# Adjacency attention in seven-product units: where the shared product stands, and in which order the tiles of a pass come

## Reference

```python
h = jnp.maximum(_layernorm(x, axis=-1), 0.0)            # x: 4096 x 512
q = h @ Wq.T + bq; k = key @ Wk.T + bk; v = value @ Wv.T + bv
scores = jnp.einsum('nd,md->nm', q, k) / 4096 ** 0.5
adj_scores = scores * adj                               # adj: 4096 x 4096 of 0 and 1
adj_scores = jnp.where(jnp.abs(adj_scores) < 1e-05, -1000000000.0, adj_scores)
prob = jax.nn.softmax(adj_scores, axis=-1)
out = x + jnp.einsum('nm,md->nd', prob, v) @ Wm.T + bm
```

## Time and profile before

| what | value |
|---|---|
| runs | 1549.62, 1549.89, 1547.48 us; median 1549.62 |
| profiled execution, its own time | 1546.85 us |
| its span, first to last instruction | 1545.0 us |
| PE busy | 1522.7 us, 99%, 7064 matmuls in the records |
| DVE, ACT, POOL busy | 1061.2, 633.7, 217.9 us |
| granted PE clock | 1.000 of full speed, mean |
| DMA | 283.24 MB, 183 GB/s mean |

### The profile page before, as it was taken

The page is one execution under the profiler, slowest core; times in us unless marked ns, Lnnn a source line. Parts: engine busy times, 40 slices in busy tenths (PEclk is TensorE's granted clock), DMA queues, the critical chain, the costliest instruction groups (busy, mean ns, idle before and its releaser), DMA issues.

```text
span 1545.0 us, 23780 instructions
## 1 busy us (share of the span) xinstructions
PE 1522.7 (99%) x7064; PEld 700.5 (45%) x7064; DVE 1061.2 (69%) x2191; ACT 633.7 (41%) x1040; POOL 217.9 (14%) x291
## 2 busy tenths in 40 slices
PE   8998999999999999999999999999999999999998
PEld 5543444444444444444444444444444444444444
DVE  5989777766667666666766666676666767676662
ACT  5776433434343333334333334343333434333332
POOL 6164000020020101002010010201001020200100
PEclk9999999999999999999999999999999999999999
DMA  9834786678868687686868768676866868787664
GB/s 346 280 78 98 184 200 154 155 194 217 200 164 205 150 229 173 168 209 157 206 155 231 173 162 210 154 211 163 223 171 162 212 149 216 170 211 174 147 163 109
DMA packets 459508, 283.24 MB, mean 183 GB/s; under 512 B 377411, under 2 KB 385859, under 8 KB 459334
## 3 DMA queue, kind: packets, MB, share of 16 engines
q1 hardware_dynamic: 459456, 282.67, 72.7%
q10 hardware_dynamic: 6, 0.01, 0.0%
HBM read 175.38 MB, written 15.73 MB: 124 GB/s over the span
## 4 chain that ended last, share of the span: by engine, by line
PE 92%; DVE 3%; ACT 2%; DMA 2%; issue 1%; SPq 0%; ACTq 0%; DVEq 0%
PE R L833 15%; PE R L835 15%; PE R L834 15%; PE S L833 11%; PE S L835 11%; PE S L834 11%; PE M L833 3%; PE M L835 3%; PE M L834 3%; PE R L951 1%; PE R L904 1%; DMA pT<-ph 0%; DMA Kbuf<-key_factors 0%; DVE Vbuf L1581 0%; DMA pT<-osb 0%
## 5 line engine op out<-in xcount | busy, mean ns | idle before, releaser
L1293 ACT ACTIVATE drop<-Zbuf 128x512 f32<-128x512 f32 x256 | 161.1, 629 | 687.9 <-DVE cmx L1605 557.7
L833 PE MATMUL R<-Vbuf,pT 128*128 128x512 f16 x1008 | 382.1, 379 | 4.8 <-DMA pT<-ph 2.4
L835 PE MATMUL R<-Vbuf,pT 128*128 128x512 f16 x1008 | 382.0, 379 | 0.0
L834 PE MATMUL R<-Vbuf,pT 128*128 128x512 f16 x1008 | 382.0, 379 | 0.0
L833 PE MATMUL S<-Kbuf,qT 128*128 128x512 f16 x738 | 279.7, 379 | 0.0
L834 PE MATMUL S<-Kbuf,qT 128*128 128x512 f16 x738 | 279.7, 379 | 0.0
L835 PE MATMUL S<-Kbuf,qT 128*128 128x512 f16 x738 | 279.7, 379 | 0.0
L1657 DVE SCALAR_TENSOR_TENSOR Zbuf<-S,rs,adjb 128x512 f32<-128x512 f32 x178 | 133.5, 750 | 210.2 <-PE S L835 199.8
L1605 DVE CUSTOM_DVE_ANT_0 Zbuf<-drop,Zbuf 128x512 f32<-128x512 f32 x256 | 178.2, 696 | 0.0
L833 PEld LDWEIGHTS R<-Vbuf,pT 128*128 128x128 f16 x1008 | 98.6, 98 | 125.8 <-DMA pT<-ph 4.9
L835 PEld LDWEIGHTS R<-Vbuf,pT 128*128 128x128 f16 x1008 | 98.6, 98 | 118.9
(11 more groups left out here) (277 smaller groups left out, 1828.7 us busy)
## 6 DMA issues: line engine op xcount, KB each, us to landing
Kbuf<-key_factors SPq DMA_DIRECT2D x134, 512.0 KB, 4.2
adjb<-in_adj_dram SPq DMA_DIRECT2D x256, 256.0 KB, 2.9
xq<-in_x_dram SPq DMA_DIRECT2D x32, 256.0 KB, 2.8
Kbuf<-in_L_gnn_key_dram SPq DMA_DIRECT2D x8, 1024.0 KB, 13.7
xr<-in_x_dram SPq DMA_DIRECT2D x32, 256.0 KB, 3.0
out_dram<-xr SPq DMA_DIRECT2D x31, 256.0 KB, 4.3
Vbuf<-in_L_gnn_value_dram SPq DMA_DIRECT2D x7, 1024.0 KB, 7.9
key_factors<-early SPq DMA_DIRECT2D x32, 128.0 KB, 2.3
```

The lines of the kernel that those rows point to most:

```text
L833: nc.tensor.matmul(ps, lhs[0], rhs[0], start=start, stop=False, skip_group_check=added)
L834: nc.tensor.matmul(ps, lhs[0], rhs[1], start=False, stop=False, skip_group_check=added)
L835: return nc.tensor.matmul(ps, lhs[1], rhs[0], start=False, stop=stop, skip_group_check=added)
L1293: nc.scalar.activation(drop[:, :], tile_of(s.i, s.j), ACT.Abs).then_inc(abs_ready, 1)
```

## The change

The order of the tiles in a pass is new, first row, second row, and the order in which the second row's probabilities are used. The shared product T2 moves from a unit's first step to its second, ahead of T1, and with it VectorE's addition of W[0]; the units stand in the same steps. The left sums begin in step 0, each full row with a wait of its own, and s1, s2 are handed over ahead of s4, s3; ScalarE and VectorE make their halves in two parts (`low_of_mixes`), the first low half at the end of step 2, the second ahead of step 3's scores. The load of (0, "T4") moves from the end of SP's step 7 to the start of step 8. The late products use the banks W[0] and S[0] as before, with a wait on scores two steps old also for the first unit's. The factors are made in bank M0 instead of W[0]. `kept` is renamed `common`.

```diff
-        FIRST_ORDER, SECOND_ORDER = [0, 1, 2, 3, 5, 4, 7, 6], [4, 0, 5, 1, 6, 2, 7, 3]
-        SECOND_PROBS = [4, 5, 6, 7, 0, 1, 2, 3]
+        FIRST_ORDER, SECOND_ORDER = [0, 1, 3, 2, 5, 4, 7, 6], [4, 2, 5, 3, 6, 0, 7, 1]
+        SECOND_PROBS = [3, 2, 5, 4, 7, 6, 0, 1]
+        KEPT_TWO = {(0, "B11"): 0, (0, "T2"): 1, (1, "B11"): 2, (1, "T2"): 3}
+        TURNS_TWO = {4: [(0, "B21"), (1, "B21"), (0, "T3"), (1, "T4")], 5: [(0, "T1"), (1, "T1"), (0, "T4")],
+                     6: [(0, "B22"), (1, "B22"), (1, "T3")]}
-        XF = W[0]
+        XF = M0
+        LATE = [W[0], S[0], S[1]]
...
+        def factor_at(s, what):
+
+            found = KEPT_TWO.get((s.w, what))
+            if found is not None:
+                return found, None
+            q = next(q for q in RING_Q if (s.w, what) in TURNS_TWO[q])
+            return q, 16 * (len(TURNS_TWO[q]) * s.nth + TURNS_TWO[q].index((s.w, what)) + 1)
...
+                    if s.j == 8:
+                        wait(sp, unit_mm, 3 * s.before + 6)
+                        load_factor((0, "T4"), 5)
+                        wait(sp, scores_done, s.t)
+                        load_factor((1, "T3"), 6)
...
-                if s.strassen and s.j == 7:
-                    wait(sp, unit_mm, 6 * s.nth + 6)
-                    load_factor((0, "T4"), 5)
...
             def row_mixes(i):
...
+                    wait(pool, q_in, 16 * (2 * i + p))
+                    wait(pool, p_lo, PASS * (i - 1) + NC - 2)
                     nc.gpsimd.tensor_tensor(full, hi, lo, ALU.add).then_inc(s_steps, 1)
...
+                wait(pool, p_lo, PASS * (i - 1) + NC)
+                wait(pool, s_steps, 3 * nth + 2)
                 nc.gpsimd.tensor_tensor(s1, a21, a22, ALU.add).then_inc(s_steps, 1)
-                nc.gpsimd.tensor_tensor(s3, a11, a21, ALU.subtract)
...
+                wait(pool, s_steps, 3 * nth + 3)
+                nc.gpsimd.tensor_tensor(s2, s1, a11, ALU.subtract).then_inc(s_made, 1)
+                wait(pool, s_made, 2 * nth + 1)
+                nc.gpsimd.tensor_tensor(s4, a12, s2, ALU.subtract)
+                nc.gpsimd.tensor_tensor(s3, a11, a21, ALU.subtract).then_inc(s_made, 1)
...
-                if s.strassen and s.j == 1:
+                if s.strassen and s.j == 0:
                     row_mixes(s.i)
...
                     elif s.unit == 0:
                         wait(pe, z1_ready, s.t - 1)
                         pe.wait_ge(kept_in, 16 * 4)
-                        unit_product(S[s.j % 2], qT[:, 0, :, 0:2, :], 2 * s.w, True).then_inc(unit_mm, 1)
-                        pe.wait_ge(kt_lo, 2 * len(PIECES))
-                        wait(pe, s_ready, s.nth + 1)
-                        unit_product(W[0], qS[:, :, 2:4, :], 2 * s.w + 1, True).then_inc(unit_mm, 1)
+                        unit_product(S[s.j % 2], qT[:, 0, :, 0:2, :], factor_at(s, "B11")[0], True).then_inc(unit_mm, 1)
                     elif s.unit == 1:
                         wait(pe, z1_ready, s.t - 1)
-                        wait(pe, kr_in[5], 48 * s.nth + 16 * (s.w + 1))
-                        unit_product(S[s.j % 2], qS[:, :, 0:2, :], 5, True).then_inc(unit_mm, 1)
+                        wait(pe, s_ready, 2 * s.nth + 1)
+                        unit_product(W[0], qS[:, :, 2:4, :], factor_at(s, "T2")[0], True).then_inc(unit_mm, 1)
+                        unit_product(S[s.j % 2], qS[:, :, 0:2, :], landed_factor(s, "T1"), True).then_inc(unit_mm, 1)
...
                         if s.unit == 0 and m == 1:
-                            wait(pe, kr_in[4], 64 * s.nth + 16 * (s.w + 1))
-                            wait(pe, p1_ready, NU * s.nth + s.w + 1)
-                            unit_product(S[s.j % 2], qT[:, 0, :, 2:4, :], 4, False).then_inc(scores_done, 1)
+                            wait(pe, p1_ready, s.count + 1)
+                            unit_product(S[s.j % 2], qT[:, 0, :, 2:4, :], landed_factor(s, "B21"), False).then_inc(scores_done, 1)
...
-                    wait(act, p_lo, PASS * (s.i - 1) + NC + 2 * s.w + 2)
+                    wait(act, p_lo, PASS * (s.i - 1) + NC + SECOND_PROBS.index(UNITS[s.w][0]) + 1)
                     nc.scalar.activation(SUM_U[s.w], S[s.j % 2][:, :], ACT.Copy).then_inc(p1_ready, 1)
...
-                    wait(act, s_made, s.nth + 1)
-                    nc.scalar.activation(qS[:, 0, :, :].rearrange("p s n -> p (s n)"), mixes, ACT.Copy).then_inc(s_hi, 1)
+                    for k in range(2):
+                        wait(act, s_made, 2 * s.nth + k + 1)
+                        nc.scalar.activation(qS[:, 0, 4 * k:4 * k + 4, :].rearrange("p s n -> p (s n)"), mixes[:, k * CW:(k + 1) * CW], ACT.Copy)\
+                            .then_inc(s_hi, 1)
...
+            def low_of_mixes(s, k):
+
+                wait(dve, s_hi, 2 * s.nth + k + 1)
+                high, low = [qS[:, h, 4 * k:4 * k + 4, :].rearrange("p s n -> p (s n)") for h in range(2)]
+                nc.vector.tensor_tensor(low, mixes[:, k * CW:(k + 1) * CW], high, ALU.subtract).then_inc(s_ready, 1)
...
-                if s.unit == 0:
-                    wait(dve, p1_ready, NU * s.nth + s.w + 1)
-                    wait(dve, unit_mm, 6 * s.nth + 3 * s.w + 2)
+                if s.unit == 1:
+                    wait(dve, p1_ready, s.count + 1)
+                    wait(dve, unit_mm, 3 * s.count + 2)
                     nc.vector.tensor_tensor(SUM_U[s.w], W[0][:, :], SUM_U[s.w], ALU.add).then_inc(mixed, 1)
...
+                if s.strassen and s.j == 3:
+                    low_of_mixes(s, 1)
                 if s.has_scores:
...
-                if s.strassen and s.j == 3:
-                    wait(dve, s_hi, s.nth + 1)
-                    nc.vector.tensor_tensor(qS[:, 1, :, :].rearrange("p s n -> p (s n)"), mixes,
-                                            qS[:, 0, :, :].rearrange("p s n -> p (s n)"), ALU.subtract).then_inc(s_ready, 1)
...
+                if s.strassen and s.j == 2:
+                    low_of_mixes(s, 0)
```

More of the change, by code:

```diff
@@ L410, in __init__ @@
                 self.in_slot = NC * (j // NC) + (self.g if fixed and i == 1 else (FIRST_ORDER, SECOND_PROBS)[j // NC].index(self.g))
[L411 to L417, removed]
+                self.strassen = self.has_scores and (not fixed or i >= TWO_FROM)
+                order = [0, 1] if self.strassen else []
+                firsts = {g: (w, n) for w in order for n, g in enumerate(UNITS[w])}
+                seconds = {g: (w, 3 - n) for w in order for n, g in enumerate(UNITS[w])}
+                self.w, self.unit = (firsts if j < NC else seconds).get(group_at(i, j), (0, None))
+                self.nth = i - TWO_FROM
+                self.before = 0
+                if self.strassen:
+                    self.before = len(order) * (i - TWO_FROM)
+                if self.unit is not None:
+                    self.count = self.before + order.index(self.w)
+                    lates = [n for n in range(NC, j) if group_at(i, n) in seconds]
+                    self.y_before = 3 * self.before + (order.index(self.w) if j < NC else len(order) + len(lates))
                 self.prefetch = self.strassen and (not fixed or i < NPASS - 1)
@@ L468, in unit_of @@
         def unit_of(t, b, p, k):
-            return unit[:, b, k:k + 1] if own(t, b) else kept[:, 3, k:k + 1]
+            return unit[:, b, k:k + 1] if own(t, b) else common[:, 3, k:k + 1]
         def limits_of(s):
             at = [rs[:, s.p, k, s.g // 2:s.g // 2 + 1] for k in (1, 2)]
-            return at if own(s.t, s.b) else [kept[:, k, s.g // 2:s.g // 2 + 1] for k in (1, 2)]
+            return at if own(s.t, s.b) else [common[:, k, s.g // 2:s.g // 2 + 1] for k in (1, 2)]
         def last_out(s):
@@ L548, in step @@
                     h_T(s)
[L549 to L556, removed]
-                if s.strassen and s.j == 7:
[L558 to L566, removed]
+                if s.strassen:
+                    if s.j == 5:
+                        wait(sp, scores_done, s.t)
+                        load_factor((1, "B21"), 4)
+                    if s.j == 6:
+                        wait(sp, unit_mm, 3 * s.before + 3)
+                        load_factor((1, "T1"), 5)
+                        wait(sp, scores_done, s.t)
+                        load_factor((1, "B22"), 6)
+                    if s.j == 7:
+                        sp.wait_ge(kt_stored, 16 * 32)
+                        wait(sp, scores_done, s.t)
+                        load_factor((0, "T3"), 4)
+                    if s.j == 8:
+                        wait(sp, unit_mm, 3 * s.before + 6)
+                        load_factor((0, "T4"), 5)
+                        wait(sp, scores_done, s.t)
+                        load_factor((1, "T3"), 6)
+                    if s.j == 9:
+                        wait(sp, scores_done, s.t)
+                        load_factor((1, "T4"), 4)
                 if s.has_scores and s.more_adj:
@@ L617, in step @@
                 if s.making is not None:
```

(9 more changed lines are left out.)

62 lines of the change are left out of this document (23 added, 39 removed).

## The result

The changed kernel takes 1576.88 us (median of 4 runs, 1576.43 to 1578.78), the kernel before 1548.62 beside it (1547.48 to 1549.89): ratio 1.0185, 95% interval 1.0167 to 1.0202. The change costs 28 us. The forecast was 1565 within 1556 to 1574: the side was right, the size too small.

A forecast was written before the change was run, and what follows sets the result against it. TensorE's number of products was taken to bound the kernel; new waits ahead of B21, 13.6 us in eleven passes, 2.8 in the first and 0.8 in the last, sum to 17.2, giving 1565 us, range 1556 to 1574.

The forecast's parts named there:

- the second unit: Second unit of each pass: B21 waits 0.62 us for ScalarE's copy, which stands behind an absolute value.
- So the copy keeps its place: Second unit: the copy still runs from 908.56 to 909.14, since the VectorE and TensorE work ahead is unchanged.
- the first unit: First unit of each pass: B21 waits 0.62 us for the copy, between 0.42 and 1.22.
- The chain of 4.59 us: First unit: from L1657 (later L1681) through row sums, row copy and ScalarE's copy to B21 takes 4.59 us.
- set 0.36 beside its own number: First unit: by the skill's rule the low half waits for GpSimd's bias add, making L1657 0.36 us late.
- the first pass: First pass with units: late halves put B21 at 355.3; its first unit loses 2.2 us, the pass 2.8.
- The last pass: Last pass: two copy waits, 1.24 us, less the old 0.4 us factor wait, so 0.8 us.
- The shorter chain gives nothing: Rival, first unit: low halves delay step 3's scores as L1689 did; 1572.7 to 1575.4 us, chance 0.12.
- VectorE bounds the second step: Rival: sums over 0.65 us late, B22 waits 0.3 in every unit; 1571.9 to 1574.6 us, chance 0.05.
- Covered: Rival: B21 doesn't wait for the copy, only two old waits go; 1544.9 to 1547.6 us, chance 0.06.
- floor only: Rival: 0.62 plus 0.24 us per pass, no first-pass loss; 1556.1 to 1558.8 us, chance 0.08.

The follow-up runs named there:

- e2: Changed kernel with six probability products instead of three ahead of B21: 1561.16 us, ratio 1.0080 to the kernel before.
- e3: Changed kernel with nine probability products instead of three ahead of B21: 1549.05 us, ratio 1.0005 to the kernel before.
- e4: Changed kernel with the shared product T2 put back into the unit's first step: 1550.09 us, ratio 1.0009 to the kernel before.
- e1: Changed kernel with the old order of the second row's probabilities put back: 1570.25 us, ratio 1.0134 to the kernel before.
- e6: Changed kernel with GpSimd's bias add of the output row held back to step 4's scores: 1579.48 us, ratio 1.0196 to the kernel before.
- e8: Changed kernel with both low halves behind the low half of the probabilities in step 3: 1585.99 us, ratio 1.0239 to the kernel before.
- e5: Kernel before with only the new orders of tiles and probabilities: 1549.21 us, ratio 1.0002.
- e10: Changed kernel, three products still ahead of B21, with the old probability order and both low halves behind step 3's row sums: 1563.19 us, ratio 1.0091.

## Why the prediction was right and wrong

**Right: what limits, and how.** TensorE's products set the time, their number didn't change, and nearly all of the cost is a wait for ScalarE's copy ahead of each B21, since three products don't cover copy and hand-offs. e2, e3 and e4 show it in doses. That B22, the factor loads and the longer second step cost nothing held too.

**Wrong: the second unit, "So the copy keeps its place".** This is the step that failed. It named the one instruction ahead of the copy in its queue, and forgot the copy's own wait. The copy overwrites a slot that still holds a probability tile, so it waits for the low half of tile 7 of the pass before. In the old order that tile is the fourth, in the new one the fifth (SECOND_PROBS.index, plus 1, in the diff): its low half is made one step later, in the step right ahead of the copy, which so starts at 925.93 instead of right behind the absolute value (924.74 + 0.54, by e1's rows). With the old order put back the gap is 0.61, as forecast; so the term was sound but for this wait. 11 x 0.67 = 7.4 of the 11.1 us that the forecast's sum lacked are here.

**Undersized: the first unit.** 0.75 to 0.81 in place of 0.62, 1.8 us in eleven passes. The chain of 4.59 us was exact in each of its parts; L1681 was 0.36 late instead of 0.2. Two things hold the low halves. One is the high halves, behind an exponential that starts late; e6 shows that they are enough alone. The other is L1736, 1.49 us with GpSimd's bias add beside it: it ends at 906.45 + 1.49 = 907.94, and the first low half starts at 907.90 with no idle time ahead of it. That L1736 would be enough alone is read from these rows; no run moved the high half and left the bias add. The exponential is late by L1628, which took 1.05 us with GpSimd's sums beside it and 0.68 in the next step, when GpSimd was idle; no run took the sums away, so this cause is argued. The prediction had set 0.36 beside its own number, from the Trainium skill (SBUF — State Buffer, "Who interferes with whom"); the number agrees with the trace, but by luck: e6 shows that the bias add alone, which that sentence blamed, doesn't make it.

**Undersized: the first pass.** The fall of the clock behind the long wait, 1.7 us, was not in the sum. The waits came to 2.4 us over before (forecast 2.8), but this nearness hides two misses: the first unit's was 3.29 - 1.91 = 1.4 in place of 2.2, since B21 came at 355.37 (355.3 foretold) while B11 was 0.9 later than before, and the second unit's was 1.03 in place of 0.62. The last pass lost 0.3 in place of 0.8, and 1.1 us of waits for landed rows had been put at nothing; what makes these is open.

**The rivals.** "The shorter chain gives nothing" is refuted by e8: without the early halves the gap is 1.39. "VectorE bounds the second step" is refuted: no gap stands before B22. "Covered" and "floor only" fell with the gaps. The time of the rival with no gain from the shorter chain (1572.7 to 1575.4) was closest, by other causes.

## What to carry to other kernels

When a cover is cut from nine products to three, list all that the covered instruction waits for, its own semaphores as well as its queue, in the new order: a wait that had been met a step earlier becomes the one that ends last. An edit that is free in one place (e5) is paid in full in another, so its price belongs to the cover that is left and not to the edit. And a wait of a few microseconds on TensorE is to be priced with what its clock does afterwards.

## What the runs showed of the hardware

In the profiled executions the granted clock fell to the lower level behind the first pass's wait in seven of these kernels and not in the others, and not by the wait's length alone: behind 2.3 us in e10 it fell, behind 2.7 us in e4 it didn't. The tables by stretches, first e10, then e4:

```profile
352.00:356.00 4.00, 1.89 (x6) 0.69 (x6) 2.73 (x8) 1.69 (x3) 0.00 (x0) 0.77 0.94 217
356.00:360.00 4.00, 4.00 (x17) 1.62 (x16) 2.51 (x5) 1.56 (x2) 0.00 (x0) 0.81 0.43 158
```

```profile
354.00:356.00 2.00, 0.05 (x1) 0.00 (x0) 1.11 (x5) 0.93 (x3) 0.00 (x0) 1.00 0.63 175
356.00:358.00 2.00, 1.40 (x7) 0.70 (x8) 0.75 (x1) 1.06 (x3) 0.00 (x0) 1.00 1.01 220
```

Where it fell, 7 to 14 products came slower, most of them 0.43 us from start to start instead of 0.22. Nor does the kernel alone seem to decide it: over a whole execution the mean granted clock is 0.999 in three of e3's ten and in four of e4's ten and 1.000 in the others, and 1.000 in one of four of e2 and of e10, where the other three have 0.999. What decides it stays open. The Trainium skill (TensorE: Matmul & The Clock Gate, "HAM oscillation — how this bites in real kernels") tells of such a fall behind waits for data; the changed kernel's row of 0.57 agrees with that.
